# Row maximum of an attention kernel: two transposes, a copy and a spread give way to two DMAs over a DRAM scratch

## The reference

```python
h = jnp.maximum(_layernorm(x), 0.0)
q, k, v = h @ Wq.T + bq, h @ Wk.T + bk, h @ Wv.T + bv
a = q @ k.T / 16 + adj + adj          # 4096 x 4096
out = x + softmax(a, axis=-1) @ v
```

## Time and profile before

| | |
|---|---|
| median of 3 runs | 823.91 us |
| the profiled execution | 823.64 us |
| its span, first to last instruction | 821.8 us |
| PE busy | 807.6 us (98%), 6702 matmuls |
| DVE busy | 587.8 us (72%) |
| POOL busy | 382.8 us (47%) |
| ACT busy | 361.2 us (44%) |
| granted clock of PE | 1.00 of full speed |
| DMA share of 16 engines | 33.2% on SP's queue |

### The profile page before, as it was taken

How to read it: one execution, slowest core, us unless ns; L and a number is a source line. 1 busy time by engine, 2 the same in 40 slices (tenths; PEclk the granted TensorE clock), 3 DMA queues, 4 the chain that set the end, 5 groups by cost and what they waited for, 6 DMA issues and landing times.

```text
span 821.8 us, 16591 instructions
## 1 busy us (share of the span) xinstructions
PE 807.6 (98%) x6702; PEld 805.4 (98%) x6702; DVE 587.8 (72%) x980; ACT 361.2 (44%) x651; POOL 382.8 (47%) x329
## 2 busy tenths in 40 slices
PE   7899999999999999999999999999999999999998
PEld 6899999999999999999999999999999999999988
DVE  4687777677777777777777777777777777777753
ACT  3684434434443343444334444434444444444364
POOL 2463908263360727346071724618182451818272
PEclk9999999999999999999999999999999999999999
DMA  6350324334332433334243333323333332333200
GB/s 223 114 182 26 104 78 129 91 91 116 91 109 72 130 92 99 106 91 116 67 126 101 93 104 92 115 76 118 103 91 111 90 108 83 111 103 98 84 26 14
DMA packets 43852, 81.68 MB, mean 99 GB/s; under 512 B 4992, under 2 KB 5632, under 8 KB 43776
## 3 DMA queue, kind: packets, MB, share of 16 engines
q1 hardware_dynamic: 43344, 80.10, 33.2%
q10 hardware_dynamic: 432, 0.53, 0.2%
HBM read 76.42 MB, written 4.19 MB: 98 GB/s over the span
## 4 chain that ended last, share of the span: by engine, by line
PE 97%; DVE 1%; ACT 1%; DMA 1%; issue 0%; POOL 0%; ACTq 0%; DVEq 0%
PE ps L309 50%; PE ps L395 15%; PE ps L397 15%; PE ps L396 15%; PE ps L301 1%; DMA w_all<-in_w 1%; PE ps L382 0%; PE ps L375 0%; ACT x_third L460 0%; PE ps L328 0%; PE ps L324 0%; DVE x_res L620 0%; DVE hT L562 0%; POOL v L263 0%; ACT v_full L478 0%
## 5 line engine op out<-in xcount | busy, mean ns | idle before, releaser
L309 PE MATMUL ps<-qhl,hT 128*128 128x256 f32 x3072 | 407.5, 282 | 1.2 <-POOL v L263 1.2
L309 PEld LDWEIGHTS ps<-qhl,hT 128*128 128x128 f32 x3072 | 384.4, 190 | 1.4 <-POOL v L263 1.4
L281 POOL TENSOR_TENSOR ring_a<-ring_a,m_row 128x512 f32<-128x512 f32 x179 | 230.2, 1332 | 215.4 <-ACT m_row L523 215.4
L395 PE MATMUL ps<-v,p_hi 128*128 128x258 f32 x1024 | 291.1, 284 | 1.2 <-DVE x_res L620 1.2
L397 PE MATMUL ps<-v,p_lo 128*128 128x258 f32 x1024 | 288.9, 282 | 0.0
L396 PE MATMUL ps<-v,p_hi 128*128 128x256 f32 x1024 | 288.7, 282 | 0.0
L519 ACT CAST p_hi<-ps 128x512 fp32r<-128x512 f32 x256 | 150.4, 588 | 246.3 <-PE ps L397 244.2
L577 DVE TENSOR_TENSOR ring_a<-ps,ring_a 128x512 f32<-128x512 f32 x179 | 123.4, 689 | 102.3 <-PE ps L309 101.5
L395 PEld LDWEIGHTS ps<-v,p_hi 128*128 128x128 f32 x1024 | 194.0, 189 | 1.4 <-DVE x_res L620 1.4
L397 PEld LDWEIGHTS ps<-v,p_lo 128*128 128x128 f32 x1024 | 194.1, 190 | 0.0
L396 PEld LDWEIGHTS ps<-v,p_hi 128*128 128x128 f32 x1024 | 193.3, 189 | 0.0
(11 more groups left out here) (74 smaller groups left out, 362.9 us busy)
## 6 DMA issues: line engine op xcount, KB each, us to landing
ring_a<-in_adj SPq DMA_DIRECT2D x179, 256.0 KB, 2.7
ring_b<-in_adj SPq DMA_DIRECT2D x77, 256.0 KB, 2.7
x_res<-in_x SPq DMA_DIRECT2D x16, 256.0 KB, 3.0
out<-x_res SPq DMA_DIRECT2D x16, 256.0 KB, 2.0
x_pair<-in_x SPq DMA_DIRECT2D x5, 512.0 KB, 3.8
x_third<-in_x SPq DMA_DIRECT2D x2, 512.0 KB, 3.7
w_all<-in_w ACTq DMA_DIRECT2D x2, 256.0 KB, 3.9
x_pair<-in_x SPq DMA_DIRECT2D x4, 128.0 KB, 4.0
```

Source lines behind the costliest of these rows:

```text
L281: nc.gpsimd.tensor_tensor(slot_tiles(w), slot_tiles(w), m, ALU.subtract).then_inc(s_sub, 1)
L309: last = nc.tensor.matmul(dst, lhs(a, ib), rhs(c, ib), start=(n == 0), stop=(n == 3 * DB - 1))
L395: nc.tensor.matmul(ps[:, O_BANK + i, 0:VW], hi, v[:, n, 0:VW], start=(n == 0), stop=False)
```

## The change

The second pair of transposes (`spread_max` on PE) and the copy (`keep_max` on ACT) go. DVE's last small operation no longer spreads: it subtracts on 128 x 2 numbers and writes them to `row_max`. SP writes those 256 numbers to a DRAM scratch, waits until that DMA has landed, and reads the scratch back into all 128 partitions of `m_row`. The scratch has two buffers. In the scratch, query i*128 + p stands at place i*128 + p, so the two numbers of one partition lie 512 bytes apart.

```diff
+        max_spill = [nc.dram_tensor(f"max_spill{n}", [QS, P], f32, kind="Internal").ap() for n in range(2)]
...
+            def spread_max(b):
+                sp.wait_ge(s_rows, b + 1)
+                sp.dma_start(max_spill[b % 2].rearrange("i p -> p i"), row_max[:, :],
+                             allow_slow_non_contiguous=True).then_inc(s_spill, 16)
+                if b >= 2:
+                    sp.wait_ge(s_sub, UNITS * (b - 1))
+                sp.wait_ge(s_spill, 16 * (b + 1))
+                sp.dma_start(m_row[:, b % 2], bass.AP(max_spill[b % 2].tensor, 0, [[0, P], [1, QB]])).then_inc(s_m, 16)
...
-            for s in range(RING, STEPS + UNITS):
-                if s < STEPS:
+            for s in range(FIRST + 4, STEPS + UNITS):
+                if RING <= s < STEPS:
                     load_adj(s)
+                if s % UNITS == 4:
+                    spread_max(s // UNITS - 1)
+                if s < RING:
+                    continue
...
-                    pool.wait_ge(s_m, b + 1)
+                    pool.wait_ge(s_m, 16 * (b + 1))
...
-            def spread_max(b):
-                pe.wait_ge(s_rows, b + 1)
-                for i in range(QS):
-                    last = nc.tensor.transpose(ps[:, X_BANK, i * P:(i + 1) * P], max_rows[:, i, :], ident[:, :])
-                last.then_inc(s_bcast, 1)
...
-            def keep_max(b):
-                act.wait_ge(s_bcast, b + 1)
-                nc.scalar.copy(m_row[:, b % 2], ps[:, X_BANK, 0:QB]).then_inc(s_m, 1)
...
                     if b > 0:
-                        dve.wait_ge(s_bcast, b)
+                        dve.wait_ge(s_turn, b)
...
             def reduce_max(b):
                 dve.wait_ge(s_turn, b + 1)
+                if b > 0:
+                    dve.wait_ge(s_spill, 16 * b)
...
-                wide = [a.rearrange("p (i one) -> p i one", one=1).broadcast_to([P, QS, P])
-                        for a in (row_shift[:, :], term)]
-                nc.vector.tensor_tensor(max_rows[:, :, :], wide[0], wide[1], ALU.subtract).then_inc(s_rows, 1)
+                nc.vector.tensor_tensor(row_max[:, :], row_shift[:, :], term, ALU.subtract).then_inc(s_rows, 1)
```

More of the change, by code:

```diff
@@ L52, in graph_attention_kernel @@
         row_shift = sb("row_shift", [P, QS])
-        max_rows = sb("max_rows", [P, QS, P])
+        max_cols = sb("max_cols", [P, QS, P])
         m_row = sb("m_row", [P, 2, QB])
@@ L161, in graph_attention_kernel @@
         s_rows = sem("row_max_spread")
-        s_bcast = sem("row_max_broadcast")
+        s_spill = sem("row_max_spilled")
         s_m = sem("row_max_in_rows")
@@ L374, in turn_max @@
                 for i in range(QS):
-                    last = nc.tensor.transpose(ps[:, X_BANK, i * P:(i + 1) * P], max_rows[:, i, :],
+                    last = nc.tensor.transpose(ps[:, X_BANK, i * P:(i + 1) * P], max_cols[:, i, :],
                                                ident[:, :])
                 last.then_inc(s_turn, 1)
-            def spread_max(b):
-                pe.wait_ge(s_rows, b + 1)
-                for i in range(QS):
-                    last = nc.tensor.transpose(ps[:, X_BANK, i * P:(i + 1) * P], max_rows[:, i, :], ident[:, :])
-                last.then_inc(s_bcast, 1)
             def weigh_values(w):
@@ L428, in _ @@
                     turn_max(b - 1)
-                if u == 1 and b <= BLOCKS:
-                    spread_max(b - 1)
                 if u == UNITS // 2 and b + 1 < BLOCKS:
@@ L528, in _ @@
                     write_p_hi(due(s) + 1)
-                if u == 1 and b <= BLOCKS:
-                    keep_max(b - 1)
                 if s not in HOLD and 0 <= due(s) + 2 < STEPS:
@@ L591, in running_max @@
                     if b > 0:
-                        dve.wait_ge(s_bcast, b)
+                        dve.wait_ge(s_turn, b)
                     halves = acc[:, :].rearrange("p (k i n) -> p k i n", k=KT, i=QS)
-                    nc.vector.tensor_tensor(max_rows[:, :, :], halves[:, 0], halves[:, 1], ALU.max)\
+                    nc.vector.tensor_tensor(max_cols[:, :, :], halves[:, 0], halves[:, 1], ALU.max)\
                         .then_inc(s_cols, 1)
```

## The result

| | before | after |
|---|---|---|
| median | 823.18 us (4 runs) | 893.85 us (889.37 to 901.42, 4 runs) |
| ratio, 95% interval | | 1.0872 [1.0821, 1.0923] |
| profiled execution, span | 823.64, 821.8 us | 901.42, 899.6 us |
| PE busy | 98% | 93% |
| mean granted clock of PE | 1.000 | 0.952 |

What follows compares the result with a forecast made beforehand. PE was taken to bound the kernel. 3.15 us from removed transposes plus 0.11 us gained in block 0 gave 3.26 us: 820.65 us against the median, range 819.4 to 823.2 us.

Steps and rivals of the forecast that it cites:

- What bounds the kernel: Whole kernel: PE is 97% of the chain of waits and issues matmul behind matmul through the middle.
- the 0.21 us: PE time per block freed by removing the second transposes; 3.15 us in all without block 0.
- the rival that it would not come back: PE finds another wait in each block, or only the first pair costs: 823.5 us, chance 8%.
- The store: SP's write of 256 numbers to the DRAM scratch: 2.0 us, ends 1.2 and 4.1.
- The second rival: Each 4-byte piece of the scratch store is dear, over 0.28 us: slower, 828.1 us at D = 8.5; chance 9%.
- The first rival: Each 4-byte write first reads what it changes, 1.3 us more, D = 5.3: 822.0 us, no change; chance 25%.
- The load: SP's broadcast read of the scratch into `m_row`: 2.0 us, ends 1.3 and 3.9.
- the trip D: From DVE's small subtract to the landed `m_row`, store plus load: 4.0 us, ends 2.5 and 8.0.
- The formula in D: Kernel time = 823.91 - 3.15 + (D - 4.1), plus (D - 5.6) beyond 5.6, for blocks 0 and 15.
- nothing is paid: Blocks 1 to 14: D up to 8.9 us is free before DVE notices, leaving 4.9 us of cover at 4.0.
- SP's hold: Blocks 1 to 14: SP held 2.0 us by the store, adjacency loads behind it having 4.7 us spare; no cost.
- The clock: PE's granted clock was at full speed in all 40 slices before; no term for a lower one.

Runs made afterwards that it cites:

- experiment 10: Changed kernel with 8-byte pieces, blocks 0 and 15 keeping both transposes and the copy (the mixed version): 818.73 us, ratio 0.9953.
- experiment 2: Kernel before with more single DMAs (the probes) behind its last store; only landing times read: load of the place just written 5.0 us, another place 2.9 us.
- Experiment 8: Changed kernel with its 4-byte pieces written 512 bytes apart and the row loaded from `bv` instead of the scratch: 820.66 us, ratio 0.9977.
- Experiment 5: Changed kernel with each partition's two numbers adjacent in the scratch, 128 pieces of 8 bytes, issued from SP: 825.61 us, ratio 1.0039.
- experiment 3: Kernel before, keeping transposes and copy, plus both DMAs on SP with nobody but SP waiting for them: 889.54 us, ratio 1.0808.
- experiment 4: Changed kernel with both DMAs issued from GpSimd instead of SP: 923.79 us, ratio 1.1246.
- experiment 7: Changed kernel with dummy transposes on PE before each block's first value product, where PE stood idle: 866.41 us, ratio 1.0530.
- experiment 9: Changed kernel with 4-byte pieces in blocks 1 to 14 only, blocks 0 and 15 keeping transposes and copy: 865.30 us, ratio 1.0513.

## Why the prediction was wrong

**What bounds the kernel, and the 0.21 us: right.** The gain per pair comes back in full where nothing is paid for it (experiment 10), so the rival that it would not come back is out.

**The store, taken as 2.0 us with ends 1.2 and 4.1: wrong, and the root.** It takes 8.2 us. I bounded it by stores of rows of 2 KB and took the number of pieces as a small addition. No row of before had pieces of a few bytes written side by side into DRAM, so the high end of 4.1 us was the slowest row of another sort, and no bound. The second rival was of the right kind and had 9%, but its price was sized by the wrong thing, the number of pieces: 128 pieces take 8.2 us as well, and 256 that lie apart 2.2 us. The first rival, a trip more for small pieces at 1.3 us, is too small for the packed ones and not there for those that lie apart.

The fixed part of about 2.0 us that I took from the Trainium skill ("DMA: Bandwidth & Descriptors", "Anatomy of one DMA") is given there for DMAs issued from GpSimd. Here, from SP, a store of one row of 1 KB took 1.1 us in all, and the store of packed pieces goes far beyond either figure. The Trainium skill's rule that transfers below 512 bytes are read, modified and written (the same page, "Specifications") has no size. The runs show no penalty for packed pieces of 64 or 32 bytes (1.6 and 1.4 us, against 1.6 at 512); it grows from there, with 2.0 us at 16 bytes, 3.6 at 8 and 8.2 at 4. But 4-byte pieces 64 bytes apart take 1.4 us, which a penalty by size alone doesn't give.

**The load, taken as 2.0 us with a high end of 3.9: wrong.** It takes 5.1 us: 2.9 us is the broadcast alone, and 2.1 us more appears when it reads what 4-byte pieces have just written (experiment 2). With the two together the trip D in the middle was 13.1 us instead of 4.0.

**The formula in D: right while D is short.** Experiment 8 gives it a D of 5.2 us, and it is off by less than the measurement can tell. Experiment 5, with a D of about 7, has its waits in blocks 0 and 15 only, as the formula says; at 7.3 it gives 824.3 us from the 822.56 us of the kernel before on that chip, and 825.61 was measured. The clock can account for the difference: it is 0.71 in the 3.4 us behind the wait in block 0.

**Blocks 1 to 14, "nothing is paid": right in the bound, wrong in what followed.** I gave DVE 8.9 us before it notices; D was 13.1 us. DVE waited 3.9 us in block 1, near 13.1 - 8.9 = 4.2, and PE 1.96 us, so PE's own free time is about 11 us. My formula had no term for this: at D = 13.3 (8.2 + 5.1) it gives 837.7 us, 56 us too few. The waits in the middle (34.3 us) and the lower clock are about that much.

**SP's hold: the wrong step that would have cost as much by itself.** I priced it with the same 2.0 us against 4.7 us to spare, and said that the loads would come earlier by more than SP is held. SP is held for 7.8 us in block 1, and the adjacency load issued right behind the broadcast load lands 5.6 us later (in experiment 3 5.3 us), where 2.7 is the median. A broadcast load ahead of it explains only 0.7 us of that by the probes; the rest stays open. Experiment 3 pays 67 us for this without a late maximum, experiment 4 over 100 us for a maximum that comes later still, without this. In the changed kernel they overlap: there is no wait of DVE for an adjacency load in its profile, since DVE is held by the maximum first.

**The clock: put at nothing, without a reason.** No rival had it, though the page showed a kernel at full clock that would now stand still in each block. Of the 70.7 us, waits of PE are 52.5 - 1.2 = 51.3, the removed transposes give back 3.4, and the rest, some 23 us by the medians and 30 by the profiled execution, is work at the lower clock; experiment 7 gets 27.4 us back by keeping PE busy, 21 to 27 of them from the clock.

## What to carry to other kernels

Before a value takes a detour over DRAM, measure that DMA by itself in the shape it will have: small pieces side by side are the costly case, and making neighbours of a partition's own numbers (4 to 8 bytes) took 8.2 us down to 3.2. Work out for each place how long the detour may take, and what stands behind the wait on the queue that issues it: here a trip of 7.3 us is free in 14 blocks and paid in the two at the ends, so the mixed version wins. A wait of PE can cost more than its length, because the clock may be lower for some microseconds behind it: it was behind all 16 waits of the changed kernel, and behind 8 of the 14 in the middle of experiment 9.

## What the runs showed of the hardware that was not expected

- A store of 4-byte pieces to DRAM takes 1.4 us for 128 pieces that lie 64 bytes apart and 8.2 us for 128 that lie packed; the trend follows the number of pieces within 256 bytes in all the forms tried.
- A load of the place that a store of packed 4-byte pieces has just written takes 5.0 us where the same load from another place takes 2.9, although the store's completion had been waited for.
- After a wait of 2.0 us PE ran at half its clock for some 3.4 us; with dummy transposes in place of the wait it did not. After a wait of 2.3 us in experiment 9 it kept its full clock, so the same length of wait can go either way.
